# Index stages of a scatter-and-mix kernel taken out of their own blocks and spread over the sweeps

## The reference

```python
center = einsum('nchw,oc->nohw', feature, w_center)       # 2 maps
step   = relu(einsum('nchw,oc->nohw', feature, w_step))   # 2 maps
prob   = sigmoid(einsum('nchw,oc->nohw', feature, w_prob))
offset = center * step
th = minimum(round(row + offset[0]), h - 1)
tw = minimum(round(col + offset[1]), w - 1)
tgt = mod(th * w + tw, h * w)                   # where each pixel writes its own coordinates
sample = grid_flat.at[tgt].set(grid_flat)       # scatter, the last writer wins
sampled = grid_sample_bilinear(feature, sample) # read the feature there
proped = sampled * prob + feature * (1 - prob)
out = feature * prob + proped * (1 - prob)
```

## Time and profile before

| what | value |
| --- | --- |
| median of 3 runs | 10036.8 us (10035.82 to 10036.99) |
| profiled execution | 10041.73 us; its span 10039.4 us |
| PE busy | 5688.7 us (57%) |
| DVE busy | 5791.8 us (58%) |
| ACT busy | 3314.3 us (33%) |
| POOL busy | 3805.1 us (38%) |

### The profile page before, as it was taken

The page is one execution under the profiler, slowest core; times in us unless marked ns, Lnnn a source line. Parts: engine busy times, 40 slices in busy tenths (PEclk is TensorE's granted clock), DMA queues, the critical chain, the costliest instruction groups (busy, mean ns, idle before and its releaser), DMA issues. The chain is left out here.

```text
span 10039.4 us, 85605 instructions
## 1 busy us (share of the span) xinstructions
PE 5688.7 (57%) x23732; PEld 2719.6 (27%) x23732; DVE 5791.8 (58%) x10809; ACT 3314.3 (33%) x6426; POOL 3805.1 (38%) x9006
## 2 busy tenths in 40 slices
PE   6841078311899988999700221888880011288888
PEld 2320033100444444444300110333330001133333
DVE  3347143571444434444389895666667989566666
ACT  5640066200444544445400000555450000054544
POOL 4530545204445544455400002666650000366665
PEclk8976589765889988899855665888895556588888
DMA  6851268513678876788710003666662000366665
GB/s 218 296 207 46 48 240 298 173 39 63 224 263 297 297 264 226 268 295 299 258 23 0 0 10 69 204 214 217 211 205 64 0 0 10 87 209 212 219 207 193
DMA packets 399395, 1675.31 MB, mean 167 GB/s; under 512 B 112501, under 2 KB 135772, under 8 KB 331621
## 3 DMA queue, kind: packets, MB, share of 16 engines
q1 hardware_dynamic: 203068, 908.43, 28.8%
q10 hardware_dynamic: 131400, 685.12, 16.8%
q0 software_dynamic: 64480, 76.57, 4.1%
HBM read 952.23 MB, written 727.72 MB: 167 GB/s over the span
## 5 line engine op out<-in xcount | busy, mean ns | idle before, releaser
L678 DVE TENSOR_TENSOR ps<-ps,arena 128x400 f32<-128x400 f32 x1600 | 929.9, 581 | 2088.6 <-PE ps L464 1161.7
L437 POOL DMA_INDIRECT arena<-table,gidx x1600 | 1616.5, 1010 | 954.6 <-issue 466.6
L457 PE MATMUL ps<-arena,minus 128*128 128x400 f32 x3200 | 1670.1, 606 | 396.0 <-DVE arena L680 260.2
L388 POOL TENSOR_TENSOR arena<-arena 128x32 f32<-128x32 f32 (+8 forms) x3450 | 808.3, 277 | 1876.2 <-issue 1066.1
L600 ACT ACTIVATE arena<-ps 128x400 f32<-128x400 f32 x1600 | 792.3, 495 | 2096.3 <-PE ps L451 1193.2
L487 PE MATMUL ps<-arena,w_conv 128*10 128x512 f32 (+1 forms) x2800 | 1205.9, 559 | 293.5 <-DMA arena<-x 283.7
L1173 POOL DMA_INDIRECT arena<-table,arena x160 | 151.9, 949 | 3137.4 <-DVEq L1208 2325.3
L606 ACT ACTIVATE arena<-iota,gcol 128x400 f32<-128x400 f32 x800 | 495.0, 619 | 2395.0 <-PEq L1208 2395.0
L540 ACT ACTIVATE arena<-ps 10x512 f32<-10x512 f32 (+1 forms) x1400 | 745.9, 540 | 1356.2 <-PE ps L487 1340.2
L500 PE MATMUL ps<-ident,arena 128*128 128x128 f32 x5000 | 844.8, 314 | 385.1 <-ACT arena L554 199.6
L1110 PE MATMUL ps<-ident,arena 128*1 128x128 f32 x4 | 1.5, 373 | 1731.3 <-DVE arena L856 1731.3
(11 more groups left out here) (195 smaller groups left out, 5357.3 us busy)
## 6 DMA issues: line engine op xcount, KB each, us to landing
arena<-x SPq DMA_DIRECT2D x200, 1600.0 KB
arena<-table SPq DMA_DIRECT2D x200, 1600.0 KB
table<-arena ACTq DMA_DIRECT2D x400, 512.0 KB, 2.7
y<-arena ACTq DMA_DIRECT2D x100, 1600.0 KB
arena<-y SPq DMA_DIRECT2D x100, 1600.0 KB
out<-arena ACTq DMA_DIRECT2D x100, 1600.0 KB
table<-arena ACTq DMA_DIRECT2D x200, 576.0 KB, 8.2
arena<-table,gidx POOLq DMA_INDIRECT x1600
```

The costliest lines, as they stand in the source:

```text
L388: last = E.tensor_tensor(tmp[:, :, at:at + size], cols[:, :, y + to:end + to:step], cols[:, :, y:end:step], ALU.subtract)
L437: pool.indirect_dma_start(got[:, m % DEPTH, e * C:(e + 1) * C], None, rows, bass.IndirectOffsetOnAxis(ap=gidx[:, 2 * m + e:2 * m + e + 1], ...
L457: nc.tensor.matmul(ps[:, 4 + r % 2, 0:W], minus[:, :], tile(t)[:, at], start=True, stop=False)
L678: V.tensor_tensor(d, d, g, ALU.mult).then_inc(s_mix, 1)
```

## The change

All index stages go into sweeps: X0 into S1, X1 into S2, X2 into S3, X3 into S4. `indices(u)` becomes a set of generators, one for each engine. `sweep` advances DVE's by one step ("piece") for each row of each tile (`pace=1.0`; in S1 0.42 of a step for a row), behind that row's mixing. Where a step waits for a DMA, empty steps (`blanks`) are put before it. The engines other than DVE place their index instructions at the row at which DVE's has been issued (`after`). The two loops over rounds stay whole: DVE and PE run them in one go, in one row. The index stage's own DMAs go from SP's queue to ACT's.

To make room, index stage and sweep have memory of their own, and PSUM banks 0 and 1 are the index stage's. The sweep keeps six: turns in 2 and 3, mixing in 4 and 5, the gate in 6 alone (two banks only in listed sweeps), the convolutions in 7 alone (in S0 and S1 in 6 and 7). Convolutions go in eight chunks of 400 instead of seven of up to 512. Table rows are loaded in halves of 4 rows (2 buffers in S2 and S3, 3 in S4 and S5) instead of whole tiles of 8 rows in 2 buffers. The turned tile is stored in 3 pieces from 2 buffers of a piece, before from 2 buffers of a whole tile. In S2 and S3 PE's first convolution of a row stands between L457 and the transposes.

Columns are blended by POOL or DVE as `owned` says: all by POOL until the index stage's DVE part is over, then by DVE for 22 tiles in S1, 11 in S2 and 3 in S3, while POOL moves columns, the rest by POOL. The list of the changed kernel: DVE's part of the index stage ends in row 227 of 400 and some in S1, 95 in S2, 342 in S3 and 342 in S4.

In S4 ("the third mixing sweep") ACT builds both images' one-hot rows (four instructions a row instead of two) and DVE none. S5 stays as it was in this.

```diff
-        sweep(0, None, 0)
-        alone_with(0)
-        sweep(1, None, 1)
-        alone_with(1)
-        sweep(2, 0, 2)
-        sweep(3, 1, 3)
-        alone_with(2)
-        sweep(4, 2, None)
-        alone_with(3)
-        sweep(5, 3, None)
+        sweep(0, None, 0, None)
+        sweep(1, None, 1, 0, pace=0.42, spell=99)
+        sweep(2, 0, 2, 1, spell=11)
+        sweep(3, 1, 3, 2, spell=3)
+        sweep(4, 2, None, 3)
+        sweep(5, 3, None, None)
...
+                def piece(ins, name=None):
+
+                    note(ins, name)
+                    yield
+                    dve.wait_ge(s_v, n[0])
...
+                compare(0)
+                for i in range(SIDE * SIDE):
+                    dve.wait_ge(s_v, loop0 + 2 * i + 1)
+                    if i + 1 < SIDE * SIDE:
+                        compare(i + 1)
+                    else:
+                        dve.wait_ge(s_v, n[0])
+                    note(V.tensor_tensor(near, near, hit[i % 2], ALU.max))
+                    yield
...
+            GB = 2 if listed else 1
+            CB = 1 if mixing else 2
...
+            def owned(t):
+
+
+                if u_idx is None and not mixing:
+                    return "pool" if t % 2 else "dve"
+                now = (t + behind) * BROWS + 3
+                return "dve" if "moved" in born and now <= born["moved"] + BROWS * spell else "pool"
...
+                    clock = [0]
+                    work = vector(dve, clock)
                     for t in range(ROUNDS):
                         for r in range(BROWS):
+                            slot = clock[0] = t * BROWS + r
                             if mixing and here(t):
                                 mix(t, r)
-                            if r == 3 and tabling and here(t - behind) and blends("dve", t - behind):
-                                blend_columns(dve, V, t - behind)
+                            if r == 3 and tabling and here(t - behind):
+                                owner[t - behind] = owned(t - behind)
+                                if owner[t - behind] == "dve":
+                                    blend_columns(dve, V, t - behind)
                             if r == 3 and tabling and here(t - behind - 1):
                                 blend_rows(t - behind - 1)
+                            if int((slot + 1) * pace) > int(slot * pace):
+                                next(work, None)
...
+                            for j in (2 * t, 2 * t + 1):
+                                if j >= RR:
+                                    sp.wait_ge(s_sxp, u_mix * H + HALF * (j - RR + 1))
+                                    alone(sp, "sp")
...
                         nc.tensor.matmul(ps[:, 4 + r % 2, 0:W], minus[:, :], tile(t)[:, r * W:(r + 1) * W], start=True, stop=False)
+                        if r < PAIRS and tabling and here(t - behind):
+                            conv(t - behind, 2 * r)
```

More of the change, by code:

```diff
@@ L26 @@
 COLS = BPX // PX
[L27 to L29 removed]
+NEARBY = 4
+BLANKS = 6
+CHUNKS = [(at, W) for at in range(0, BPX, W)]
+PAIRS = len(CHUNKS) // 2
+HALF = BROWS // 2
 TURNED = [(j, min(4, COLS - j)) for j in range(0, COLS, 4)]
@@ L228, in build @@
+        tops = again(halo_at, BROWS * SLOTS, NB)
+        stage = again(halo_at, STAGE * C)
+        near_at = used[0]
         near = part(BPX, NB, F16)
+        code = near
         hit_at = used[0]
         hit = [part(BPX, NB, F16) for _ in range(2)]
-        hot = [[again(hit, hit_at + (4 * i + j) * (W // 2), W, 128, F16) for j in range(4)] for i in range(2)]
-        zrow = code[0:RMAX, 0:W]
-        codes = part(SIDES[-1] ** 2 + 1)
+        lsrc, ltmp, lpos = (again(near_at + a * BROWS * SLOTS, BROWS * SLOTS, NB) for a in range(3))
@@ L816, in vector @@
-                step(V.memset(far, 0.0))
-                dve.wait_ge(s_gatest, (u + 1) * 16 * 6)
-                step(V.memset(near, 0.0))
-                yield
+                yield from piece(V.tensor_copy(parts[0], z))
+                yield from piece(V.tensor_tensor(z, z, parts[0], ALU.subtract))
+                yield from piece(V.tensor_copy(parts[1], z))
+                yield from piece(V.tensor_tensor(z, z, parts[1], ALU.subtract))
+                yield from piece(V.tensor_copy(parts[2], z), "gate")
@@ L821, in vector @@
+                step(V.scalar_tensor_tensor(s1m, s0m, 1.0, z, ALU.add, ALU.mult), "far")
+                step(V.memset(halo[:, :, 0:RMAX], 0.0))
+                step(V.memset(halo[:, :, RMAX + W:], 0.0), "halo")
+                yield from blanks(BLANKS)
+                dve.wait_ge(s_codest, (u + 1) * 16 * 4)
+                yield from piece(V.memset(far, 0.0))
+                yield from piece(V.memset(near, 0.0))
+                yield from blanks(2)
                 dve.wait_ge(s_halo, (u + 1) * 16 * 6)
@@ L1070, in sync @@
+                nc.scalar.activation(z, z, ACT.Square, bias=half[0:NB, 0:1]).then_inc(s_zact, 1)
+                yield from after(act, clock, "gate")
                 for i in range(2):
                     for j, t in enumerate((near, *hit)):
-                        sp.dma_start(gates[u][3 * i + j].rearrange("(b e) -> b e", b=BLK),
-                                     each(t.bitcast(BF16))[i]).then_inc(s_gatest, 16)
-                yield
-                sp.wait_ge(s_v, mark["code"])
+                        act.dma_start(gates[u][3 * i + j].rearrange("(b e) -> b e", b=BLK),
+                                      each(t.bitcast(BF16))[i]).then_inc(s_gatest, 16)
@@ new lines, in _ @@
+                    clock = [0]
+                    work = tensor(pe, clock)
+                    for t in range(ROUNDS):
+                        for r in range(BROWS):
+                            clock[0] = t * BROWS + r
+                            if mixing and here(t):
+                                row(t, r)
+                            elif r < PAIRS and tabling and here(t - behind):
+                                conv(t - behind, 2 * r)
+                            if r < PAIRS and tabling and here(t - behind):
+                                conv(t - behind, 2 * r + 1)
+                            if tabling and here(t - 2):
+                                for g in turns_at(r):
+                                    turn(t - 2, g)
+                            if r == BROWS - 1 and tabling and here(t - 2) and t - 2 in LATE:
+                                turn_late(t - 2)
+                            next(work, None)
@@ L1222, in _ @@
+                    clock[0] = 10 ** 9
+                    for _ in work:
                         pass
@@ new lines, in _ @@
+                    clock[0] = 10 ** 9
+                    for _ in work:
+                        pass
+                    if tabling:
+                        n = (u_tab + 1) * TILES
+                        for a in range(2):
+                            act.wait_ge(s_cst[a], n * PAIRS // 2 * 16)
+                            act.wait_ge(s_tst[a], n * len(PIECES) // 2 * 16)
+                        act.wait_ge(s_lst, (u_tab + 1) * len(LATE) * 16)
+                    if mixing:
+                        for a in range(FR):
+                            act.wait_ge(s_yst[a], (TILES - a + FR - 1) // FR * 16)
```

1275 lines of the change are left out of this document (649 added, 626 removed).

## The result

The changed kernel takes 9894.0 us (median of 4 runs, 9866.9 to 9914.7) against 10036.9 before: ratio 0.985, 95% interval 0.9832 to 0.9868. The forecast was 8195, its range 7880 to 8750. The kernel is faster, but by 1.5% where 18% were forecast. The windows of the six sweeps of the kernel after stand beside the earlier trace rows; their columns are the same.

What follows compares the result with a forecast made beforehand. Two bounds in turn, DVE in index stages and PE in sweeps, each idle meanwhile. Removing four index blocks (3608 us) left S0 to S5 at 668 + 742 + 1614 + 1910 + 1958 + 1304 = 8196, said as 8195 us; range 7880 to 8750.

Steps and rivals of the forecast that it cites:

- what the small buffers cost: S0: the third piece's copy waits for the first's store, 0 to 2 us a tile; 20 us added, giving 668.
- signs of being wrong: Among them: ACT's copies or stores are what PE waits for; S1 exceeds 850 us through POOL's blends or the pace.
- Rival 2: Reduced buffering costs more: S2, S3 convolutions wait 0.7 us, S0 and S1 lose 2 us a tile; 8680; chance 0.11.
- the sentence on POOL's moves: X2's and X3's column moves by POOL come from row 342 on and end within their sweeps; no size given.
- X0's steps ... fit beside it: S1: some 3.4 index steps a tile at 2.8 us fit beside the sweep, DVE being 37% busy.
- Rival 4: DVE and POOL block each other: 62 us in S4, some 15 in S3 and S2; 8275; chance 0.05.
- its term: S1 at 742 us: blends 353 and 249, start 15, first loop 90, rounds of the second 35.
- Rows without a step: S2 has 305, S3 and S4 58 each; 3.35 us a row in S2 and S3, 3.4 in S4.
- rival 3: S2's and S3's 404 rows without a full slot run at 2.63 us, not 3.35: 291 less, 7905; chance 0.10.
- A round of the first loop: Index loop run whole inside the sweep, nothing of the sweep going on: 96 us a round, 16 more than before.
- rival 1: PE falls to the low clock in full slots of S2 to S4: 8465, or 8915 at clock 0.50; chance 0.18.
- Rival 5: Half-tile table loads come late in S2 and S3: 12.6 us for each of 200 halves, 10715, slower; chance 0.03.

Runs made afterwards that it cites:

- c4b: The changed kernel with four buffers instead of two for the convolution maps on their way out, nothing else; 8675.2 us, ratio 0.8622.
- c4ordb: The changed kernel with four conv-map buffers and POOL's move of far columns put behind the last blend that POOL owes; 8421.4 us, ratio 0.8376.
- alonec4: The changed kernel with pace 0 in S1 to S4 (index stages alone behind their sweeps) and four conv-map buffers; 9826.6 us, one run.

## Why the prediction was wrong

The step that failed is the one on what the small buffers cost. The prediction wrote "Two store buffers of a piece: the third piece's copy waits until the first is stored, 2.7 us after issue", put 20 us on it for S0, and looked at the table's stores alone. The conv maps' stores, cut from two a tile to four and with two buffers of a pair, have no term in the sum at all. They cost 911 us (c4b): 5.2 us a tile in S0, 3.4 in S1, 6.6 in S2, 3.2 in S3. Two of the prediction's own signs of being wrong came: ACT's copies and stores are what PE waits for, and S1 exceeds 850 us. Rival 2 named the reductions in buffering, with 2 us a tile for S0 and S1 and a mechanism (copy and wake-up) that was not the one at work; it gave 8680. The duration of the earlier trace rows, 2.7 us for a table store of 512 KB, was not that of a conv-map store of 31 KB, which frees its buffer after 6.3 us in S0 (median of its 49 waits) and 11.7 in S2, because larger stores stand in ACT's queue in front of it.

The second is the sentence on POOL's moves, "X2's and X3's moves by POOL fall into rows 342 and on, and end in their sweeps". True, but POOL's queue holds a tile that it still has to blend behind X1's and X2's moves: 254 us by the totals of c4b and c4ordb (193 in S2 and 80 in S3, less what other stages vary).

The third is S1's "X0's steps ... fit beside it, for DVE is 37% busy". DVE has room for them (49% busy in S1 of c4ordb), but POOL's blend stands still meanwhile. Rival 4 had the exclusion, but priced it on DVE's side only (62 us in S4) and by the row of DVE's L648; POOL pays more. S1 stays 303 us over its term in the best kernel, of which 141 go with the steps. POOL pays in S4 too: a gather's POOL instruction takes 947 ns in the earlier trace rows's stage, 961 in S4 of alonec4, where no step runs beside it, and 1843 beside index steps (kernel after, 6700 to 7700 us, 432 of them), hidden there behind DVE's row.

```profile
L1104 POOL DMA_INDIRECT arena<-table,gidx x432 | 796.1, 1843 | 162.0 <-issue 129.2 <-PE ps L1147 32.8
```
```profile
L437 POOL DMA_INDIRECT arena<-table,gidx x749: 941/947/1462, 6300.1 to 7498.8; - x188
```

What held, in c4ordb, where these two are mended: S2 1707 (forecast 1614), S3 1951 (1910), S4 1915 (1958). Rows without a step are 3.3 to 3.4 us apart in S2 and S3 by their median, as forecast, so rival 3 had no part there; S2's mean is 3.5, which makes some 40 of its 93 us. Part of the agreement in S4 is luck, for its errors cancel. Rows with a comparison are 3.9 us apart in S3 and 4.34 in S4 by their median (forecast 4.2 and 4.9): DVE's five instructions take 4.63 us by their durations but start 4.34 apart, since four of them begin 0.07 to 0.1 us before the one ahead has ended. A round of the first loop takes 82 us, not 96, and S4's rows behind the last step are 2.5 us apart, not 3.4. Against these gains stands X3's move by POOL in S4, which holds up the gathers, so that PE waits 86 us in one row; the forecast had no term for it. PE is granted 0.82 to 0.86 in 100 us windows of S3's full slots and 0.74 to 0.76 in S4's, not 0.50, and DVE is busy 93% to 99% in them: rival 1 did not come about. Rival 5 did not either; no half of a table row is what PE waits for. S0 has 50 us left over its 668; ACT's waits for table stores are 60 us in it, but what they cost was not tested.

S5's 1304 held on the chip of the result and on none of the four others, where kernels with the same S5 had 1047 to 1258.

## What to carry to other kernels

When a change halves a buffer or cuts a store into smaller ones, price each ring of buffers by itself: time from issue to free, divided by the distance of its uses, tells how many buffers it needs. Take the time from issue to free in the queue as it will be: here a small store waited behind the large ones issued before it. Whether another queue for the small stores would have done as well as more buffers was not tried. When work is hidden beside other work, look at what the second engine, which is not busy with it, does meanwhile: here DVE's steps stopped POOL for their whole length, and POOL's queue put a long move ahead of a short blend that everybody waited for. Compare kernels on one chip: here a stage with no edit in it was between 1047 and 1304 us long.

## What the runs showed of the hardware that was not expected

- A store of 31 KB from ten partitions moves its packets within 0.4 us but frees its buffer 6.3 us after its issue when the last piece of a table store (576 KB) is in front of it in ACT's queue, 11.7 us with a store of 1.6 MB there too, and 5.5 us with no store in front and the loads of x at 441 GB/s beside it; a table store of 512 KB took 2.7 us in the trace before.
- POOL's elementwise instructions wait for the whole of a DVE instruction with two SBUF inputs (3.49 us) or a TENSOR_SCALAR (1.83 us for the same 3200 columns) but not for MAX8; a gather's POOL instruction takes twice as long beside such steps (947 and 961 ns without, 1843 with).
- The same program has its S5 at 1051, 1243 or 1304 us on three chips, while the kernel before, with the same work in whole-tile loads, takes 10033 to 10052 us in all on each of five. The cause is open.
